# Attention heads on one core: TensorE makes the maxima's products, then the product of the weights with v, then the transposed scores

## The chip, the cores and the metric

The kernel runs on one core of a Trainium2 chip. The metric is device time in microseconds (us), lower is better. Five engines of the core matter: TensorE (PE, matrix products into PSUM), VectorE (DVE), ScalarE (ACT), GpSimd (POOL) and SyncE (SP, which issues the DMAs). Each works through its own list of instructions in order and waits on semaphores for the others. TensorE's clock has two levels here, 1.2 and 2.4 GHz; the profile gives the granted one as a share of full speed.

## What is computed

Two transformer-like layers over x of 4 x 1024 x 256, in float32, each half followed by a layer norm of x plus the half's output: a gated convolution with an MLP, a mixture of experts, an attention with block mask and rotary positions, and a gated MLP that keeps the two largest of each four hidden values. The change is in the attention alone:

```python
q = _rope(q)                      # (B=4, H=16, T=1024, D=16)
k = _rope(k)
scores = jnp.einsum('bhqd,bhkd->bhqk', q, k) * SCALE
scores = jnp.where(tok_mask[None, None], scores, -jnp.inf)   # blocks of 64, causal
attn = jax.nn.softmax(scores, axis=-1)
ctx = jnp.einsum('bhqk,bhkd->bhqd', attn, v)
ctx = ctx.transpose(0, 2, 1, 3).reshape(Bc, Tc, Cc)
return ctx @ w_o.T
```

## The kernel before

The program has three phases: convolution and MLP, experts, then attention and the last MLP. The third (`attention_ffn_phase`) handles the four sequences one after the other: `heads(b)` makes the attention of sequence b, then the output projection and the MLP of b follow, among which the projections and the first maxima of sequence b+1 are spread. Nothing of the MLP can begin before `heads(b)` has given the whole context.

In `heads(b)` the 16 heads are taken in four groups g = 0..3 of four heads. A group has 20 steps s, two for each of ten units of the score matrix (`UNITS`): the even step is heads 0 and 1 of the group (pair 0), the odd step heads 2 and 3. A unit is up to four blocks of 128 x 128; unit 2 (steps 4 and 5) and unit 9 (steps 18 and 19) are two blocks wide. Four kinds of work belong to a step:

- `scores(b, g, s)` (L1841): TensorE makes k times q, that is the transposed scores, for one pair, into the PSUM bank `W[s % 2]`. It waits (`exp_ok`) until ScalarE has read that bank two steps earlier. Scores are made one step ahead: in step s those of s+1.
- `exponentials(b, g, s)` (L1382): ScalarE takes exp of the bank and writes it to SBUF, into the unit's slot of `weights`.
- `weighted(b, g, u, part)` (L1861): TensorE multiplies v by the weights of unit u = s/2 - 1, for all four heads, and adds it up in the bank `O`. It is called in the even steps 2, 4 .. 18 for the unit whose second exp is that of step s-1, and waits for that exp. The last unit's product is made in step 0 of the next group, or after the loop in the last group. Here it is called "the product with v".
- `for_maxima` (L1814, L1817): q times k for another group, whose row maxima VectorE takes (`maximum`, L1543 and L1548). Two jobs in a step, through the two halves of the bank `X`; a job waits until VectorE has read its half. The jobs done in group g are those of group g+1, and from step 17 on those of g+2 (`max_jobs`). Group 0's own jobs are made ahead of `heads`, so group 2 has none after step 16 and group 3 has none at all.

In odd steps there is something more on TensorE: transposes of q and k rows of later groups (L1781), which ScalarE then copies out (L1372, L1376), or of the sums (`sums_transposed`, L1870), whose copy by ScalarE is L1388 (after exp 0 and exp 7) and which VectorE divides out.

The order is written out by hand. Before the change TensorE's step is: scores of s+1, two maxima jobs, the extra work of an odd step, and in an even step the product with v last. In step 0 it is already: product with v of the group before, maxima jobs, scores. ScalarE's order in a step is exp of s, then copies; it is not touched, nor is VectorE's.

Of the kernel before, what the change touches and what calls it, by code (L numbers as in the profile page):

```python
# [61 lines left out]
def wait(eng, sem, value):  # L62

    if not isinstance(value, int) or value > 0:
        eng.wait_ge(sem, value)  # L65
# [1036 lines left out]
NHG = HEADS // HG  # L1102
# [44 lines left out]
def attention_ffn_phase(nc, io, keep):  # L1147
    with ExitStack() as ctx:  # L1148
# [114 lines left out]
        def group(b, g):  # L1263

            return Step(None, 0, b * NHG + g)
# [5 lines left out]
        def max_jobs(g, s):  # L1271

            return (g + 1, AHEAD + 2 * s) if AHEAD + 2 * s < 2 * NX else (g + 2, AHEAD + 2 * s - 2 * NX)
# [477 lines left out]
        def _(pe):  # L1751
# [32 lines left out]
            def qk_transposed(b, g, pair, s):  # L1784
                rows_transposed(t_bank(g, pair, s), g, pair, s, kq_mm)

            def q_max_transposed(b, g, pair):
                wait(pe, nm_ok, group(b, g)(2, LEAD + pair + 1))
                rows_transposed(q_max_bank(g, pair), g, pair, 0, tm_mm)
# [33 lines left out]
            def for_maxima(b, g, low, high):  # L1823
                for m in range(low, high):
                    for_maximum(b, g, m)
# [47 lines left out]
            def heads(b):  # L1873
                scores(b, 0, 0)
                qk_transposed(b, 1, 0, 1)
                wait(pe, qm_ok, group(b, 0)(2, 1))
                qk_transposed(b, 1, 0, 0)
                for_maxima(b, 1, 0, AHEAD)
                q_max_transposed(b, 0, 1)
                for g in range(NHG):  # L1880
                    for s in range(STEPS):
                        of, m = max_jobs(g, s)
                        if s == 0 and g > 0:
                            weighted(b, g - 1, NU - 1, 0)
                        if s == 0 and of < NHG:
                            for_maxima(b, of, m, m + 2)
                        if s + 1 < STEPS:
                            scores(b, g, s + 1)
                        elif g + 1 < NHG:
                            scores(b, g + 1, 0)  # L1890
                        if s > 0 and of < NHG:
                            for_maxima(b, of, m, m + 2)
                        if s == 1 and g > 0:
                            wait(pe, qm_ok, group(b, g)(2, 2))
                            sums_transposed(b, g - 1, 1)
                        if s == 9:
                            if g + 1 < NHG:
                                wait(pe, kq_ok, group(b, g + 1)(4, 4))
                            elif g > 0:
                                wait(pe, cn_ok, group(b, g - 1)(2, LEAD + 2))  # L1900
                            sums_transposed(b, g, 0)
                        if g + 1 < NHG:
                            if s == 3:
                                if g > 0:
                                    wait(pe, cn_ok, group(b, g - 1)(2, LEAD + 2))
                                qk_transposed(b, g + 1, 1, 1)
                            if s == 5:
                                wait(pe, kq_ok, group(b, g + 1)(4, 3))
                                qk_transposed(b, g + 1, 1, 0)
                            if s == 11:  # L1910
                                wait(pe, cn_ok, group(b, g)(2, LEAD + 1))
                                q_max_transposed(b, g + 1, 0)
                        if g + 2 < NHG:
                            if s == 13:
                                wait(pe, qm_ok, group(b, g + 1)(2, 1))
                                qk_transposed(b, g + 2, 0, 1)
                            if s == 15:
                                wait(pe, kq_ok, group(b, g + 2)(4, 1))
                                qk_transposed(b, g + 2, 0, 0)
                        if s > 0 and s % 2 == 0:  # L1920
                            weighted(b, g, s // 2 - 1, 0)
                        if s > 0 and s % 2 == 0:
                            weighted(b, g, s // 2 - 1, 1)
                        if s == STEPS - 1 and g + 1 < NHG:
                            if g + 2 < NHG:
                                wait(pe, kq_ok, group(b, g + 2)(4, 2))
                            else:
                                wait(pe, qm_ok, group(b, g + 1)(2, 1))
                            q_max_transposed(b, g + 1, 1)
                weighted(b, NHG - 1, NU - 1, 0)  # L1930
                wait(pe, cn_ok, group(b, NHG - 1)(2, LEAD + 1))
                sums_transposed(b, NHG - 1, 1)
# [212 lines left out]
```

How the kernel before makes its waits and increments, by code:

```python
def wait(eng, sem, value):  # L62
    if not isinstance(value, int) or value > 0:
        eng.wait_ge(sem, value)
# [110 lines left out]
        def x_arrived(eng, n, par):  # L176
            if n.reg is None:
                eng.wait_ge(x_loaded[par], 16 * (n.off // 2 + 1))
            else:
                eng.wait_ge(x_loaded[par], n.reg * 16 + 16 * (n.off // 2 + 1))
# [1 line left out]
        @block.sync  # L183
# [11 lines left out]
            sp.dma_start(got_dn, io["w_dn"]).then_inc(dn_ld, 16)  # L195
            sp.dma_start(got_out, io["w_out"]).then_inc(out_ld, 16)
            for n, par in steps(sp, 2, ALL):
                if n.among(1, NG):
                    wait(sp, xx_ok, n(1))
                    load(n.before(-1), 1 - par)
                if n.among(1, NG + 1):
                    b = n.before(1)
                    wait(sp, xa_ok, b(1, 1))
                    sp.dma_start(io["rows_t"][:, tiles(b), 0:D], x2).then_inc(row_st, 16)
            sp.wait_ge(row_st, 16 * NG)
# [1 line left out]
        @block.gpsimd  # L207
        def _(pool):
            pool.memset(power[:], -0.5).then_inc(setup, 1)
            pool.memset(eps[:], 1e-5).then_inc(setup, 1)
            pool.wait_ge(setup, 2)
            def rms(n, ss_ok, ss, g, g_ok, rn, rn_ok, used):
# [7 lines left out]
            rms(Step(None, 0, 0), ss1_ok, ss1, g1, g1_ok, rn1, rn1_ok, h_ok)
            pool.wait_ge(wa_ok, 3)
            pool.tensor_tensor(w_up[1][:, :, :], got_up, w_up[0][:, :, :], ALU.subtract).then_inc(wp_ok, 1)
# [502 lines left out]
            def gather():  # L728
                pool.wait_ge(idx_ok, 1)
                pool.wait_ge(w_st, 16)
```

## Time and profile before

| | |
|---|---|
| median of 3 runs | 1879.51 us (1877.37 to 1886.38) |
| the profiled execution | 1887.31 us, its span 1885.2 us |
| TensorE busy | 1636.9 us (87%), mean granted clock 0.924 |
| VectorE busy | 1134.7 us (60%) |
| ScalarE busy | 798.1 us (42%) |
| steps of `heads`, four sequences, each | 116 to 117 us |

A row of the timeline is: start and length in us, engine, line, operation, what it writes and reads, shape, how many instructions were merged into the row, and in brackets the idle time of the engine before it with what ended it. PE is the matrix product itself, PEld the load of its fixed operand. ScalarE instructions overlap a little: one exp of full width lasts 1.02 us, and the next begins 0.9 us after the start of it. A row of the windows is: stretch, its length, then the busy time (and number of instructions) of PE, PEld, DVE, ACT and POOL, then the granted clock, the DMA share and GB/s.

### The profile page before, as it was taken

To read this page: it belongs to the slowest core of one execution; us is meant where nothing else is said; L and a number is where in the kernel's file an instruction comes from. 1 tells how busy PE (TensorE), PEld (TensorE's weight loads), DVE (VectorE), ACT (ScalarE), POOL (GpSimd) and SP (SyncE) were. 2 spreads that over 40 slices of the span, in tenths; PEclk is the share of its full clock that TensorE was granted. 3 is DMA by queue.
4 is the path that set the end of the run, shared out by engine and by line. 5 is a ranking of instruction groups with operands and counts; after the bars stand their busy time and mean duration, and the time that the engine had idled before them with its cause. 6 is when DMAs were issued, how large, how long until landed. Compare 5 with 4: busy or idle time off the path is not lost.

```text
span 1885.2 us, 26388 instructions
## 1 busy us (share of the span) xinstructions
PE 1636.9 (87%) x10042; PEld 1007.5 (53%) x10043; DVE 1134.7 (60%) x2355; ACT 798.1 (42%) x1308; POOL 236.0 (13%) x237
## 2 busy tenths in 40 slices
PE   3899999986989986688899989899888899899797
PEld 3788888874557774233355433355433455433355
DVE  5566566646421036767468677577677477677465
ACT  5444444421312221357643167552167552267430
POOL 4333333311320001000000000100000100000100
PEclk8999999987999888679999989999989899989999
DMA  2000000005014412000000000000000000000000
GB/s 103 12 23 23 22 22 22 22 12 178 16 35 139 130 56 92 1 1 1 1 1 1 0 1 1 24 1 1 1 1 1 23 1 1 1 1 1 23 1 23
DMA packets 27147, 47.96 MB, mean 25 GB/s; under 512 B 7312, under 2 KB 16016, under 8 KB 26256
## 3 DMA queue, kind: packets, MB, share of 16 engines
q1 hardware_dynamic: 26464, 44.74, 7.4%
q0 software_dynamic: 576, 1.77, 0.3%
q8 instruction: 70, 1.15, 0.3%
q14 instruction: 37, 0.30, 0.1%
HBM read 37.59 MB, written 9.06 MB: 25 GB/s over the span
## 4 chain that ended last, share of the span: by engine, by line
issue 59%; POOL 2%; DVE 0%; POOLq 0%; DVEq 0%
POOL rs_sb L1314 1%; POOL ve_sb L1311 0%; POOL qks_sb L1329 0%; POOL v_sb L1328 0%; DVE bn_sb L1491 0%; POOL qks_sb L1319 0%; DVE x_sb_sb L1506 0%; POOLq L1148 0%; POOLq L65 0%; POOL qks_sb L1330 0%; DVE mv_sb L1497 0%; DVEq L1148 0%; POOL v_sb L1327 0%; DVEq L65 0%; DVEq L1495 0%
## 5 line engine op out<-in xcount | busy, mean ns | idle before, releaser
L1548 DVE TENSOR_REDUCE mx_sb<-s_ps 128x1 f32<-128x512 f32 (+1 forms) x512 | 312.7, 652 | 145.1 <-PE s_ps L1817 84.7
L1382 ACT ACTIVATE room_sb<-s_ps 128x1024 f32<-128x1024 f32 (+1 forms) x320 | 280.9, 948 | 23.7 <-PE s_ps L1841 22.7
L1814 PE MATMUL s_ps<-room_sb 48*128 48x512 f16 (+3 forms) x640 | 176.2, 346 | 25.0 <-DVE mx_sb L1548 16.7
L1861 PE MATMUL cm_ps<-room_sb,v_sb 128*32 128x512 f32 (+3 forms) x1536 | 168.3, 529 | 0.8 <-ACT room_sb L1388 0.8
L1841 PE MATMUL s_ps<-room_sb 51*128 51x128 f16 (+4 forms) x1152 | 123.6, 287 | 41.8 <-ACT room_sb L1382 34.7
L1311 POOL TENSOR_TENSOR ve_sb<-mv_sb,eps_sb 128x4 f32<-128x4 f32 x24 | 5.1, 212 | 1114.4 <-DVE mv_sb L1497 1114.4
L1984 PE MATMUL cm_ps<-w_fd_sb,room_sb 128*128 128x256 f32 x512 | 130.7, 403 | 14.6 <-DVE room_sb L1627 14.6
L1841 PEld LDWEIGHTS s_ps<-room_sb 50*128 50x128 f16 (+1 forms) x1152 | 39.1, 96 | 182.1 <-ACT room_sb L1382 146.6
L1814 PEld LDWEIGHTS s_ps<-room_sb 48*128 48x128 f16 x640 | 54.4, 98 | 145.7 <-DVE mx_sb L1548 97.0
L1971 PE MATMUL s_ps<-xbT_sb,w_fg_sb 128*128 128x512 f32 x256 | 128.9, 615 | 0.8 <-ACT xbT_sb L1419 0.8
L1971 PE MATMUL s_ps<-xbT_sb,w_fu_sb 128*128 128x512 f32 x256 | 128.3, 613 | 0.0
L392 DVE SCALAR_TENSOR_TENSOR x_sb_sb<-xp_sb,conv_w_sb,x_sb_sb 128x512 f32<-128x512 f32 x96 | 108.5, 1139 | 22.8 <-ACT x_sb_sb L319 20.6
L1984 PEld LDWEIGHTS cm_ps<-w_fd_sb,room_sb 128*128 128x128 f32 x512 | 96.8, 197 | 39.2 <-DVE room_sb L1627 14.0
L398 DVE SCALAR_TENSOR_TENSOR m1T_sb<-mm_ps,m1T_sb 128x512 fp32r<-128x512 f32 x64 | 44.3, 692 | 97.2 <-ACT m1T_sb L311 97.2
L956 PE MATMUL em_ps<-xT_sb,ws_gu_sb 128*128 128x512 f32 x192 | 91.6, 623 | 8.0 <-DMA rows<-zeros 8.0
L1424 ACT ACTIVATE sgl_sb<-s_ps 128x512 f32<-128x512 f32 x64 | 38.2, 597 | 136.0 <-PE s_ps L1971 135.9
L1817 PE MATMUL s_ps<-room_sb 51*128 51x128 f16 x512 | 81.2, 235 | 9.6 <-ACT room_sb L1372 9.2
L1543 DVE TENSOR_REDUCE mx_sb<-s_ps 128x2 f32<-128x512 f32 (+1 forms) x128 | 66.3, 554 | 24.3 <-PE s_ps L1817 24.3
L479 PE MATMUL mm_ps<-h1T_sb,w_up_sb 128*128 128x512 f32 x128 | 57.6, 450 | 23.0 <-DVE h1T_sb L416 23.0
L311 ACT ACTIVATE m1T_sb<-mm_ps 128x512 fp32r<-128x512 f32 x64 | 38.1, 596 | 80.6 <-PE mm_ps L481 80.6
L479 PE MATMUL ro_ps<-w_dn_sb,m1T_sb 128*128 128x256 f32 x256 | 71.5, 279 | 0.0
L480 PE MATMUL ro_ps<-w_dn_sb,m1T_sb 128*128 128x256 f32 x256 | 71.5, 279 | 0.0
(245 smaller groups left out, 3237.6 us busy)
## 6 DMA issues: line engine op xcount, KB each, us to landing
we_gu_sb<-we_gu SPq DMA_DIRECT2D x32, 352.0 KB
we_dn_sb<-we_dn SPq DMA_DIRECT2D x32, 176.0 KB
x_in_sb<-x SPq DMA_DIRECT2D x9, 512.0 KB, 3.5
rows<-x_sb_sb SPq DMA_DIRECT2D x8, 512.0 KB, 3.0
x_sb_sb<-rows SPq DMA_DIRECT2D x2, 2048.0 KB, 11.6
out<-x_sb_sb SPq DMA_DIRECT2D x8, 512.0 KB, 2.6
xp_sb<-w_in SPq DMA_DIRECT2D x1, 1024.0 KB, 5.8
x_sb_sb<-w_up SPq DMA_DIRECT2D x1, 1024.0 KB, 7.0
```

The costliest lines, as they stand in the source:

```text
L392: dve.scalar_tensor_tensor(xc[:, c, :], xp[:, c, k:k + GTOK], conv_w[:, c, k:k + 1], xc[:, c, :], ALU.mult, ALU.add)\
L479: pe.matmul(out, of[0][at], by[0][cols], start=start, stop=False)
L480: pe.matmul(out, of[1][at], by[0][cols], start=False, stop=False)
L956: last = pe.matmul(mm[c % 4][:, :], ws_gu[:, k, col:col + P], xT[:, k, g * GTOK:(g + 1) * GTOK], start=(k == 0), stop=(k == KD - 1))
L1382: act.activation(weights[(g * NU + u) % SLOTS_P][:, 2 * pair:2 * pair + 2, 0:width(u) * P], W[s % 2][:, :, 0:width(u) * P], ACT.Exp, scale ...
L1548: dve.tensor_reduce(mx[:, pair, k % 2, slot:slot + 1], X[:, k % 2, 0:count * P], AX.X, ALU.max, negate=True).then_inc(mx_ok, 1)
L1814: last = pe.matmul(X[:, k % 2, at * P:(at + plain) * P], query[head:head + NORM, i * P:(i + 1) * P], key[head:head + NORM, j * P:(j + plai ...
L1817: last = pe.matmul(X[:, k % 2, (at + plain) * P:(at + count) * P], query[head:head + USED, i * P:(i + 1) * P], key[head:head + USED, i * P ...
L1841: last = pe.matmul(W[s % 2][:, head, (at + low - i) * P:(at + high - i) * P], key[first:first + rows, j * P:(j + 1) * P], query[first:firs ...
L1861: last = pe.matmul(O[32 * h:32 * h + 32, (i - half * GT) * P:(i - half * GT + count) * P], v[:, j, g * HG + h, :], weights[(g * NU + u) % ...
L1971: last = pe.matmul(bank[:, e, :], wt[:, k, ch * P:(ch + 1) * P], xbT[:, k, g * 512:(g + 1) * 512], start=(k == 0), stop=(k == KD - 1))
L1984: last = pe.matmul(CM[:, t // 2, (t % 2) * D:(t % 2 + 1) * D], hs[:, k % 3 * 4 + i, t * P:(t + 1) * P], w_fd[:, k % 2 * 4 + i, :], start=( ...
```

## The change

In every step s of `heads` TensorE's calls are put in one order: maxima jobs, then (in even steps after 0) the product with v, then the scores of the next step, then the extra work of the odd steps. No instruction is added or taken away, and no semaphore is changed; each wait stays with its instruction.

```diff
-                        if s == 0 and of < NHG:
+                        if of < NHG:
                             for_maxima(b, of, m, m + 2)
+                        if s > 0 and s % 2 == 0:
+                            weighted(b, g, s // 2 - 1, 0)
+                            weighted(b, g, s // 2 - 1, 1)
                         if s + 1 < STEPS:
                             scores(b, g, s + 1)
                         elif g + 1 < NHG:
                             scores(b, g + 1, 0)
-                        if s > 0 and of < NHG:
-                            for_maxima(b, of, m, m + 2)
...
-                        if s > 0 and s % 2 == 0:
-                            weighted(b, g, s // 2 - 1, 0)
-                        if s > 0 and s % 2 == 0:
-                            weighted(b, g, s // 2 - 1, 1)
```

TensorE in group 3, steps 8 to 14, before (L1841 the scores, two products a step at this width; L1861 the product with v; L1870 the transposed sums):

```order
L1861 MATMUL cm_ps<-room_sb,v_sb 32x512 x4
L1841 MATMUL s_ps<-room_sb 128x512 x2
L1870 MATMUL cm_ps<-ident_sb,room_sb 128x128 x4
L1841 MATMUL s_ps<-room_sb 128x512 x2
L1861 MATMUL cm_ps<-room_sb,v_sb 32x512 x4
L1841 MATMUL s_ps<-room_sb 128x512 x4
L1861 MATMUL cm_ps<-room_sb,v_sb 32x512 x4
```

and the same stretch of the change:

```order
L1861 MATMUL cm_ps<-room_sb,v_sb 32x512 x4
L1841 MATMUL s_ps<-room_sb 128x512 x4
L1870 MATMUL cm_ps<-ident_sb,room_sb 128x128 x4
L1861 MATMUL cm_ps<-room_sb,v_sb 32x512 x4
L1841 MATMUL s_ps<-room_sb 128x512 x4
L1861 MATMUL cm_ps<-room_sb,v_sb 32x512 x4
```

Both have two steps' scores between two products with v, but they are not the same scores: after the product of step s the list before goes on with the scores of s+2, that of the change with those of s+1.

TensorE at the start of `heads`, group 0, steps 1 and 2, before (L1814 and L1817 are a maxima job; the first three rows are the scores of step 2, made in step 1):

```order
L1841 MATMUL s_ps<-room_sb 128x128 x2
L1841 MATMUL s_ps<-room_sb 128x256 x2
L1841 MATMUL s_ps<-room_sb 128x128 x2
L1814 MATMUL s_ps<-room_sb 128x384
L1817 MATMUL s_ps<-room_sb 128x128
L1814 MATMUL s_ps<-room_sb 128x384
L1817 MATMUL s_ps<-room_sb 128x128
L1841 MATMUL s_ps<-room_sb 128x128 x2
```

and of the change, from the maxima jobs of step 1 on to the product with v of step 2:

```order
L1814 MATMUL s_ps<-room_sb 128x384
L1817 MATMUL s_ps<-room_sb 128x128
L1841 MATMUL s_ps<-room_sb 128x128 x2
L1841 MATMUL s_ps<-room_sb 128x256 x2
L1841 MATMUL s_ps<-room_sb 128x128 x2
L1814 MATMUL s_ps<-room_sb 128x384
L1817 MATMUL s_ps<-room_sb 128x128
L1814 MATMUL s_ps<-room_sb 128x384
L1817 MATMUL s_ps<-room_sb 128x128
L1861 MATMUL cm_ps<-room_sb,v_sb 32x512 x4
```

The maxima jobs of step 1 now stand ahead of the scores of step 2, and the product with v of step 2 stands ahead of the scores of step 3.

## Rows read from the trace of the kernel before

**Rows 1.** Windows of the four groups of the second sequence, and the sum of all 16.
```profile
1092.30:1126.50 34.20, 30.66 (x288) 12.02 (x288) 23.71 (x47) 23.42 (x27) 0.00 (x0) 0.85 0.01 2
1126.50:1159.90 33.40, 30.54 (x296) 12.56 (x296) 25.25 (x51) 23.94 (x29) 0.00 (x0) 0.90 0.01 1
1159.90:1189.50 29.60, 25.84 (x260) 10.17 (x260) 22.24 (x44) 22.07 (x27) 0.00 (x0) 1.00 0.00 1
1189.50:1208.40 18.90, 15.78 (x160) 4.90 (x164) 11.51 (x44) 18.03 (x23) 3.63 (x6) 1.00 0.14 57
...
sum 461.80, PE 408.93 PEld 158.16 DVE 321.45 ACT 349.63 POOL 11.68; mean PE 25.56 PEld 9.89 DVE 20.09 ACT 21.85 POOL 0.73
```
**Rows 2.** Waits of the whole run: who waited for whom, us, times, longest.
```profile
PE s_ps L1841 <- ACT room_sb L1382: 34.7, 84, 1.7
```
**Rows 3.** Timeline of group 3, second sequence.
```profile
1189.51 1.02 ACT L1382 ACTIVATE room_sb<-s_ps 128x1024 f32<-128x1024 f32 x1
...
1190.89 3.86 ACT L1382 ACTIVATE room_sb<-s_ps 128x1024 f32<-128x1024 f32 x5
...
1194.04 1.07 PE L1861 MATMUL cm_ps<-room_sb,v_sb 128*32 128x384 f32 x16
...
1195.05 0.60 PE L1841 MATMUL s_ps<-room_sb 50*128 50x512 f16 x4
1195.48 1.94 ACT L1382 ACTIVATE room_sb<-s_ps 128x1024 f32<-128x1024 f32 x2 [0.72 <-PE s_ps L1841]
...
1197.47 0.39 PE L1841 MATMUL s_ps<-room_sb 50*128 50x512 f16 x2 [0.53 <-ACT room_sb L1382]
1197.78 10.61 ACT L1382 ACTIVATE room_sb<-s_ps 128x1024 f32<-128x1024 f32 x12
...
1209.25 0.60 ACT L1388 ACTIVATE room_sb<-cm_ps 128x512 f32<-128x512 f32 x1 [0.86 <-PE cm_ps L1861]
```
**Rows 4.** Timeline of the end of group 2.
```profile
1185.27 1.06 PE L1861 MATMUL cm_ps<-room_sb,v_sb 128*32 128x512 f32 x8
...
1186.27 0.40 PE L1841 MATMUL s_ps<-room_sb 51*128 51x128 f16 x8
...
1186.60 1.08 ACT L1382 ACTIVATE room_sb<-s_ps 128x512 f32<-128x512 f32 x2 [1.26 <-PE s_ps L1841]
...
1187.93 0.62 PE L1781 MATMUL cm_ps<-ident_h_sb,qks_sb 128*128 128x128 f16 x8
...
1188.59 1.02 ACT L1376 ACTIVATE room_sb<-cm_ps 128x1024 f16<-128x1024 f16 x1 [0.91 <-PE cm_ps L1781]
```
**Rows 5.** Timeline of the first steps of group 0.
```profile
1093.36 0.61 PE L1841 MATMUL s_ps<-room_sb 51*128 51x128 f16 x6 [1.73 <-ACT room_sb L1382]
...
1094.27 0.61 PE L1841 MATMUL s_ps<-room_sb 51*128 51x128 f16 x6
1094.42 2.68 DVE L1548 TENSOR_REDUCE mx_sb<-s_ps 128x1 f32<-128x512 f32 x4 [3.03 <-PE s_ps L1817]
...
1096.30 1.93 PE L1861 MATMUL cm_ps<-room_sb,v_sb 128*32 128x512 f32 x8
```
**Rows 6.** Timeline of the first steps of group 2.
```profile
1162.42 0.40 PE L1841 MATMUL s_ps<-room_sb 51*128 51x128 f16 x6 [0.20 <-ACT room_sb L1382]
...
1163.34 1.06 PE L1861 MATMUL cm_ps<-room_sb,v_sb 128*32 128x512 f32 x8
```
**Rows 7.** Timeline of group 2, steps 4 to 6.
```profile
1166.54 1.07 PE L1861 MATMUL cm_ps<-room_sb,v_sb 128*32 128x384 f32 x16
...
1168.18 2.48 DVE L1548 TENSOR_REDUCE mx_sb<-s_ps 128x1 f32<-128x512 f32 x4 [0.65 <-PE s_ps L1814]
...
1169.84 0.64 PE L1861 MATMUL cm_ps<-room_sb,v_sb 128*32 128x256 f32 x8
```
**Rows 8.** Two stretches of group 0, columns as in Rows 1.
```profile
1099.20:1106.00 6.80, 5.72 (x62) 2.48 (x60) 5.88 (x13) 5.12 (x7) 0.00 (x0) 1.00 0.00 0
1106.00:1109.40 3.40, 3.40 (x24) 1.03 (x21) 1.46 (x3) 2.19 (x4) 0.00 (x0) 0.50 0.00 0
```

## The prediction, made before the changed kernel ran

> **What bounds the kernel now.** I read the busy times by group of heads first, then the list of waits, then the timeline of the places where the order changes. The heads take 461.8 us of the span in 16 groups, and groups 0 to 2 are not alike group 3 [rows 1]. In groups 0 to 2 TensorE is busy 87 to 91% of the time and sets the pace together with VectorE: where the products for the maxima are full width, TensorE makes two, VectorE reduces them, and TensorE can make the next two only as VectorE frees the halves. One such turn, from one product with v to the next, takes 3.30 us, in which VectorE does four reductions in 2.48 us [rows 7]. In group 3 there are no maxima. There ScalarE is busy 18.03 of 18.90 us [rows 1], and its exps stand nearly end to end [rows 3]: a pair of exps, 1.8 us, is the period of two steps. So group 3 is bound by ScalarE, as long as TensorE gives it scores in time.
>
> **Part 1, group 3: the scores come behind the product with v.** The units of cost are in [rows 3]. A full exp lasts 1.02 us and the next follows 0.9 us after its start (two in 1.94); a half-wide one takes 0.5 and lasts 0.6. TensorE starts scores 0.05 us after the exp it waits for has ended (1195.48 + 1.94 = 1197.42, then 1197.47). The product with v holds TensorE for 1.0 us (1194.04 to 1195.05); unit 2's, half as wide, I take at 0.57 (eight such instructions last 0.64 us where the wide ones last 1.07 [rows 7]). From scores to the exp on them it is 0.43 us where they stand right behind a product (1195.05 to 1195.48), and 0.31 us where TensorE was idle (1197.47 to 1197.78).
>
> In an even step s both the product and the scores of s+1 wait for the exp of s-1. Before, the scores go first, are ready 0.05 + 0.31 = 0.36 us after that exp, and the exp of s covers this; the product comes while ScalarE works. After the change the exp of s+1 can start only 0.05 + 1.0 + 0.43 = 1.48 us after the end of the exp of s-1, that is 1.02 + 1.48 = 2.50 us after its start, where ScalarE would be free after 1.80. So 0.7 us are added in each even step of full width. TensorE works in order, so nothing behind the product can serve ScalarE meanwhile.
>
> Walked through from the group's first exp at 0 (the second at 1.38, as in [rows 3], since a copy stands between them): exp 3 starts at 3.90, exp 5 at 6.41, exp 7 at 8.07 (small product), exp 9 at 11.08 (with the copy after exp 7), then every 2.50: 13.58, 16.08, 18.58, 21.08; exp 19 at 23.59 because the exp of step 18 is half as wide and covers less. It ends at 24.19. Before, the last copy begins 0.86 us after the last exp; now the product of unit 8 is out of its way, and I take 0.77: copy at 24.96, against 19.74 before (1209.25 less 1189.51). The group grows by **5.2 us**. The small waits before (0.72 us at one place) are inside this difference.
>
> **Part 2, the end of group 2.** From step 17 on there are no maxima there either. Counted from the product of step 16 (1185.27), the next group's first exp comes at 4.24 [rows 3, 4]. After the change: scores 17 at 1.0, exp 17 from 1.43 to 2.45, product with v of step 18 at 2.50 (before at once behind scores 18 and 19, at 1.33), scores 19 at 3.50, the next group's first scores at about 3.7, transposes at 4.0, their copy 0.66 later as before, 4.66, and the exp 0.92 behind it: 5.58. That is **1.3 us** more. Between groups 0 and 1, and 1 and 2, the maxima still fill this place; only one set of scores more stands ahead of the transposes, whose copy the next group waits for: about 0.25 us each, **0.5 us** together.
>
> **Part 3, the starts of the groups: a gain.** In step 1 scores 2 wait for exp 0, and the maxima jobs behind them wait too. At the start of group 0 this is large: TensorE idles 1.73 us before scores 2, and VectorE idles 3.03 us [rows 5]. After the change the maxima go ahead into this gap, VectorE has freed the halves when step 2 wants them, and the product with v of step 2 waits only for exp 1, which scores 3 follow today at 1094.27. It starts there and not at 1096.30: 2.0 us at most; I take **1.8 us**, since the rest of the stretch is then held by VectorE. In groups 1 and 2 the same step has the product at 1163.34, 0.92 us after scores 3 [rows 6]. It can gain 0 to 0.9; I take 0.5, because the sums' transposes and VectorE's division stand there: **1.0 us** for both.
>
> **Part 4, the rest of groups 0 to 2: nothing.** With maxima of full width the turn is: product, maxima pair, extra work and scores, first and second job of the next pair as VectorE frees them, product. Only the scores and the extra work change places, and their sum is hidden behind the reductions. Scores s+1 now stand behind the product, but their exp has the whole next 3.30 us turn to be ready in [rows 7]: it ends some 1.0 + 0.43 + 1.02 = 2.45 us after the product's start. If that cover were gone it would cost what group 3 pays, 0.7 us a turn. All waits of TensorE's scores for exps come to 34.7 us over the whole run [rows 2], so what could be won by hiding them is small, and a part of it lies in group 3, where it wins nothing.
>
> **Sum.** Per sequence 5.2 + 1.3 + 0.5 - 1.8 - 1.0 = +4.2 us, and four sequences 16.8 us. The heads are serial with what follows (the context must be whole), so it goes to the end unshortened. The profiled execution, 1887.3 us with a span of 1885.2, would be 1904; it lies 0.4% above the median of the runs, 1879.5, to which I add the same: **1896 us**.
>
> **Rivals.** *Faster.* The busiest engine of the heads is TensorE, 408.9 of 461.8 us, ScalarE only 349.6 [rows 1]. If TensorE is the bound throughout, letting independent maxima go before waiting scores wins back idle time. Groups 0 to 2 have 3.5 + 2.9 + 3.8 = 10.2 us of idle TensorE a sequence. This wins if more than 9.3 of these go, against the 2.8 I count (5.2 + 1.3 + 0.5 = 7.0 are lost, plus 2.3 to pass 0.5% over four sequences); all gone gives 4 x (7.0 - 10.2) = -13 us, 1867. Against it: most of that idle time is VectorE's turn. Chance 0.04. The Trainium skill, in "Perfetto Trace Analysis", section "Identifying the Most-Contended Engine", says to find the bound by occupancy and to optimise the busiest engine first; by that rule taken over the whole heads this change serves the right engine and the time falls. Taken group by group its occupancies agree with me: ScalarE leads in group 3.
>
> *Little change.* The terms on both sides come out at their kind ends: scores behind a product reach ScalarE after 0.31 and not 0.43 (ten places, 1.2 us less), the group borders between 0, 1 and 2 cost nothing, the starts gain 2.0 + 0.9 + 0.9. Then 4.0 + 1.3 - 3.8 = 1.5 a sequence, 6 us, 1885.5. Chance 0.14, with all that stays under 0.5%.
>
> *Much slower, by the clock.* In group 0 the granted clock falls to half from 1106.0 to 1109.4, after a stretch in which TensorE was busy 5.72 of 6.80 us [rows 8], and eight instructions of the product then take 1.93 us [rows 5] and not 1.06. Group 3 runs at full clock with 15.8 of 18.9 us busy (84%); changed, it would have the same work in some 24 us, 66%. If the clock falls in it, each product costs 0.87 more and the scores some 0.15, all on the path. With a third of its ten turns at half clock that is 3.4 us a sequence, 14 us in all: 1910. Chance 0.14. The Trainium skill, in "TensorE: Matmul & The Clock Gate", section "HAM oscillation", ties the fall to long idle gaps of TensorE; by it gaps of under 1.5 us as here would not bring the clock down and this rival would be out. The trace does not bear it out, since the fall of [rows 8] has no long gap before it; so I leave it its chance.
>
> **How the numbers follow.** Forecast (16.8 us, with terms off by a third to either side) 0.68; clock 0.14; little change 0.14; faster 0.04. A measurement of this kernel tells about 0.5%, 9.4 us, from no change. The range goes from 1885, the kind ends, to 1911, the clock's case. Slower by over 0.5% is forecast plus clock, 0.82; within 0.5% 0.14; faster 0.04.
>
> **What would show it.** Group 3 should take 24 us from first to last exp and not 18.9, with a wait of about 0.7 us for L1841 ahead of every second exp, and ScalarE at some 75% there; group 2 about 0.8 us longer, groups 0 and 1 about 1.6 and 0.3 shorter, and VectorE's 3.03 us wait at the start of group 0 mostly gone. If group 3's exps still stand end to end, part 1 is wrong; if groups 0 and 1 grow, or shrink by several us, part 4 is.

## The result: 0.3% slower, and where the time went

The changed kernel takes 1887.05 us (median of 20 runs, 1879.71 to 1896.07), the kernel before, on the same chip, 1881.35 us (20 runs). The ratio is 1.0032, with a 95% interval of 1.0018 to 1.0045: slower, by about 6 us and not by the 16.8 forecast, and within 0.5%. The time lies inside the range, the sign is right, and the size is little more than a third of the forecast. The profiled execution took 1881.48 us, with a span of 1879.4. Two timed runs of the whole study, one of the kernel before (2010.36 us) and one of e2 (2109.18 us), fell in a slower state and are left out of every median and ratio.

The page of the changed kernel, busy time by engine, and one group of instructions (the transposed scores):

```profile
PE 1619.0 (86%) x10042; PEld 999.1 (53%) x10043; DVE 1136.7 (60%) x2355; ACT 807.5 (43%) x1308; POOL 236.1 (13%) x237
...
L1841 PE MATMUL s_ps<-room_sb 51*128 51x128 f16 (+4 forms) x1152 | 121.8, 285 | 14.5 <-ACT room_sb L1382 7.3
```

The waits of the whole run (who waited for whom, us, times, longest), where one row has moved most:

```profile
ACT room_sb L1382 <- PE s_ps L1841: 98.3, 129, 1.9
...
PE cm_ps L1861 <- ACT room_sb L1382: 29.2, 40, 1.0
...
PE s_ps L1841 <- ACT room_sb L1382: 7.3, 8, 1.3
```

Before, the first row read 22.7 us, 26 times. ScalarE now waits 98.3 us for scores; 23.5 us of this lie in the four groups 3, where it waited 2.8 us before. TensorE waits for exps as long as it did, 29.2 + 7.3 = 36.5 us against the 34.7 of [rows 2], but now mostly in front of the product with v, for which the list of before has no such row, and the scores stand behind that product.

The windows of the four groups of the second sequence and the sum of all 16, as in [rows 1] (us; busy time and instructions of PE, PEld, DVE, ACT, POOL; granted clock; DMA share; GB/s):

```profile
1089.40:1120.40 31.00, 27.75 (x284) 11.45 (x284) 23.61 (x47) 23.98 (x28) 0.00 (x0) 0.93 0.01 2
1120.40:1151.00 30.60, 28.38 (x296) 12.07 (x296) 25.47 (x51) 24.64 (x30) 0.00 (x0) 1.00 0.01 1
1151.00:1181.20 30.20, 26.05 (x260) 10.35 (x260) 22.25 (x44) 22.60 (x28) 0.00 (x0) 1.00 0.00 1
1181.20:1205.30 24.10, 15.58 (x164) 4.99 (x164) 13.56 (x52) 18.64 (x23) 4.83 (x8) 1.00 0.11 45
...
sum 472.80, PE 402.08 PEld 158.83 DVE 328.25 ACT 359.44 POOL 14.47; mean PE 25.13 PEld 9.93 DVE 20.52 ACT 22.47 POOL 0.90
```

Group 3 has gone from 18.9 to 24.1 us at full clock, with ScalarE at 18.64 of 24.1 (77%). Group 2 went from 29.6 to 30.2 and group 1, at full clock, to 30.6 from 31.0. The heads as a whole take 472.8 us where they took 461.8 (116.4, 116.1, 113.5 and 116.1 for the four sequences, where the table of the time before says 116 to 117). The mechanism is there, then, yet the whole program gained back a large part. The timeline of group 3 shows the mechanism at its clearest:

```profile
1193.33 1.06 PE L1861 MATMUL cm_ps<-room_sb,v_sb 128*32 128x512 f32 x8 [0.32 <-ACT room_sb L1382]
1194.32 0.61 PE L1841 MATMUL s_ps<-room_sb 50*128 50x512 f16 x4
1194.76 1.94 ACT L1382 ACTIVATE room_sb<-s_ps 128x1024 f32<-128x1024 f32 x2 [0.57 <-PE s_ps L1841]
1195.83 1.07 PE L1861 MATMUL cm_ps<-room_sb,v_sb 128*32 128x512 f32 x8 [0.90 <-ACT room_sb L1382]
1196.83 0.61 PE L1841 MATMUL s_ps<-room_sb 50*128 50x512 f16 x6
1197.26 1.94 ACT L1382 ACTIVATE room_sb<-s_ps 128x1024 f32<-128x1024 f32 x2 [0.57 <-PE s_ps L1841]
```

Product, scores, two exps, a gap of 0.57 us, and again: from 1193.33 to 1195.83 it is 2.50 us a turn, to the hundredth what the prediction worked out. (The gap is 0.57 us and not 0.7 because the two exps beside it last 1.94 us, not 1.80.) In [rows 3] twelve exps stood end to end there.

The same at the start of group 0, against [rows 5]:

```profile
1088.58 0.53 PE L1814 MATMUL s_ps<-room_sb 48*128 48x384 f16 x2
...
1089.24 1.29 DVE L1548 TENSOR_REDUCE mx_sb<-s_ps 128x1 f32<-128x512 f32 x2 [0.70 <-PE s_ps L1817]
1089.43 2.85 ACT L1382 ACTIVATE room_sb<-s_ps 128x1024 f32<-128x1024 f32 x3
...
1090.51 0.61 PE L1841 MATMUL s_ps<-room_sb 51*128 51x128 f16 x6 [1.30 <-ACT room_sb L1382]
...
1091.47 1.93 PE L1861 MATMUL cm_ps<-room_sb,v_sb 128*32 128x512 f32 x8
1091.58 1.29 DVE L1548 TENSOR_REDUCE mx_sb<-s_ps 128x1 f32<-128x512 f32 x2 [1.05 <-PE s_ps L1817]
```

The maxima jobs of step 1 now run at 1088.58, before scores 2 wait; VectorE's wait of 3.03 us has become two, of 0.70 and 1.05, with two reductions between them, and the product of step 2 comes 2.04 us after exp 0 (1091.47 less 1089.43), where it came 4.0 after it (1096.30 less 1092.3).

### The profile page after: what moved, and what is told of

Read it like the earlier page. It is cut to its first block, busy times and chain, and to the rows that moved or that the text cites. A ratio compares the mean times of both kernels' runs of the same rounds, so it can differ in the third digit from the quotient of the medians.

```text
span 1879.4 us, 26388 instructions
## 1 busy us (share of the span) xinstructions
PE 1619.0 (86%) x10042; PEld 999.1 (53%) x10043; DVE 1136.7 (60%) x2355; ACT 807.5 (43%) x1308; POOL 236.1 (13%) x237
## 4 chain that ended last, share of the span: by engine, by line
issue 59%; POOL 2%; DVE 0%; POOLq 0%; DVEq 0%
POOL rs_sb L1314 1%; POOL ve_sb L1311 0%; POOL qks_sb L1329 0%; POOL v_sb L1328 0%; POOL qks_sb L1319 0%; DVE bn_sb L1491 0%; DVE x_sb_sb L1506 0%; POOLq L1148 0%; POOLq L65 0%; POOL qks_sb L1330 0%; DVE mv_sb L1497 0%; DVEq L1148 0%; POOL v_sb L1327 0%; DVEq L65 0%; DVEq L1495 0%
## 5 line engine op out<-in xcount | busy, mean ns | idle before, releaser
L1382 ACT ACTIVATE room_sb<-s_ps 128x1024 f32<-128x1024 f32 (+1 forms) x320 | 291.0, 939 | 98.7 <-PE s_ps L1841 98.3
L1814 PE MATMUL s_ps<-room_sb 48*128 48x512 f16 (+3 forms) x640 | 176.4, 345 | 33.0 <-DVE mx_sb L1548 16.4
L1861 PE MATMUL cm_ps<-room_sb,v_sb 128*32 128x512 f32 (+3 forms) x1536 | 165.7, 520 | 35.5 <-ACT room_sb L1382 29.2
L1311 POOL TENSOR_TENSOR ve_sb<-mv_sb,eps_sb 128x4 f32<-128x4 f32 x24 | 5.0, 210 | 1113.8 <-DVE mv_sb L1497 1113.8
L1814 PEld LDWEIGHTS s_ps<-room_sb 48*128 48x128 f16 x640 | 54.0, 97 | 163.6 <-DVE mx_sb L1548 98.7
L1841 PE MATMUL s_ps<-room_sb 51*128 51x128 f16 (+4 forms) x1152 | 121.8, 285 | 14.5 <-ACT room_sb L1382 7.3
L1841 PEld LDWEIGHTS s_ps<-room_sb 50*128 50x128 f16 (+1 forms) x1152 | 45.3, 97 | 133.8 <-ACT room_sb L1382 60.2
L1817 PE MATMUL s_ps<-room_sb 51*128 51x128 f16 x512 | 83.0, 233 | 10.1 <-ACT room_sb L1372 9.2
L1543 DVE TENSOR_REDUCE mx_sb<-s_ps 128x2 f32<-128x512 f32 (+1 forms) x128 | 66.2, 554 | 22.8 <-PE s_ps L1817 22.7
L1861 PEld LDWEIGHTS cm_ps<-room_sb,v_sb 128*32 128x32 f32 x1536 | 34.8, 111 | 84.0 <-ACT room_sb L1382 49.9
L479 PE MATMUL ro_ps<-w_dn_sb,m1T_sb 128*128 128x256 f32 x256 | 71.6, 280 | 0.0
```

Of the source, the lines that this page charges most:

```text
L479: pe.matmul(out, of[0][at], by[0][cols], start=start, stop=False)
L1382: act.activation(weights[(g * NU + u) % SLOTS_P][:, 2 * pair:2 * pair + 2, 0:width(u) * P], W[s % 2][:, :, 0:width(u) * P], ACT.Exp, scale ...
L1543: dve.tensor_reduce(mx[:, pair, k % 2, at:at + ST + 1:ST], X[:, k % 2, 0:2 * count * P].rearrange("p (a c) -> p a c", a=2), AX.X, ALU.max, ...
L1814: last = pe.matmul(X[:, k % 2, at * P:(at + plain) * P], query[head:head + NORM, i * P:(i + 1) * P], key[head:head + NORM, j * P:(j + plai ...
L1817: last = pe.matmul(X[:, k % 2, (at + plain) * P:(at + count) * P], query[head:head + USED, i * P:(i + 1) * P], key[head:head + USED, i * P ...
L1841: last = pe.matmul(W[s % 2][:, head, (at + low - i) * P:(at + high - i) * P], key[first:first + rows, j * P:(j + 1) * P], query[first:firs ...
```

## Experiments: which piece costs and which piece gains

All edits are against the kernel before, unless it says otherwise. The conditions are written here in their simplest form. Ratios are to the kernel before on the same chip, with 95% intervals. Lengths "at full clock" are of groups in which the granted clock reads 1.00; the time at half clock (1.2 GHz) in a stretch is twice its length times what the unrounded clock lacks of 1.

### e1: the maxima go first, the product stays last

```diff
-                        if s == 0 and of < NHG:
+                        if of < NHG:
                             for_maxima(b, of, m, m + 2)
                         if s + 1 < STEPS:
                             scores(b, g, s + 1)
                         elif g + 1 < NHG:
                             scores(b, g + 1, 0)
-                        if s > 0 and of < NHG:
-                            for_maxima(b, of, m, m + 2)
```

> One part of the change alone: the maxima jobs of steps 1 to 19 go ahead of the scores; the product with v stays last in its step. Theory A (the two parts add up; the loss sits where the product with v stands ahead of the scores and there are no maxima, the gain where maxima jobs no longer wait behind scores): group 3 as before, 18.9 us from first exp to end, group 2 not longer than before (29.6 us), groups 0 and 1 shorter by some 2 and 0.5 us at full clock, so about 1868 us (ratio 0.993) or less if the clock falls less often too. Theory B (groups 0 to 2 gained because the product with v moved, not the maxima): ratio 1.000.

Measured: 1861.37 us against 1882.8, ratio 0.9888 (0.9861 to 0.9915). No kernel of the study is faster (e5 below is level with it within the intervals); it is 1.1% faster than the one before and, by the two ratios, 1.4% faster than the full change. The windows of its groups 1 to 3, second sequence:

```profile
1122.00:1152.50 30.50, 28.31 (x296) 11.98 (x296) 25.50 (x51) 24.13 (x30) 0.00 (x0) 1.00 0.01 2
1152.50:1181.60 29.10, 25.98 (x260) 10.23 (x260) 22.25 (x44) 22.36 (x28) 0.00 (x0) 1.00 0.00 1
1181.60:1200.40 18.80, 15.73 (x158) 4.85 (x162) 11.48 (x44) 17.94 (x23) 3.62 (x6) 1.00 0.14 58
```

Group 3 is as before, group 2 half a microsecond shorter than the 29.6 of [rows 1], group 1 half shorter than its 31.0. All that the full change gains is in the half of it that moves the maxima.

### e2: the product goes first, the maxima stay behind the scores

```diff
                         if s == 0 and of < NHG:
                             for_maxima(b, of, m, m + 2)
+                        if s > 0 and s % 2 == 0:
+                            weighted(b, g, s // 2 - 1, 0)
+                            weighted(b, g, s // 2 - 1, 1)
                         if s + 1 < STEPS:
                             scores(b, g, s + 1)
...
-                        if s > 0 and s % 2 == 0:
-                            weighted(b, g, s // 2 - 1, 0)
-                        if s > 0 and s % 2 == 0:
-                            weighted(b, g, s // 2 - 1, 1)
```

> The other part alone: the product with v goes ahead of the scores in the even steps, the maxima jobs stay behind the scores. Theory A: group 3 takes 24.1 us instead of 18.9, the end of group 2 about 1 us more, groups 0 and 1 keep their starting gap; ratio 1.012 to 1.015 (about 1905 us). Theory B: group 3 loses the same 5.2 us, but groups 0 and 1 win back 2 to 3 us each, ratio 1.003 to 1.006.

Measured: 1970.41 us, ratio 1.0484 (1.0446 to 1.0522), three to four times the loss expected. So the two halves of the change don't add. The timeline of group 0, second sequence, shows why:

```profile
1142.02 1.07 PE L1861 MATMUL cm_ps<-room_sb,v_sb 128*32 128x512 f32 x8
...
1143.25 0.38 PE L1814 MATMUL s_ps<-room_sb 48*128 48x512 f16 x2
1143.66 2.48 DVE L1548 TENSOR_REDUCE mx_sb<-s_ps 128x1 f32<-128x512 f32 x4 [1.37 <-PE s_ps L1814]
1144.12 0.40 PE L1841 MATMUL s_ps<-room_sb 51*128 51x128 f16 x6 [0.49 <-ACT room_sb L1382]
1144.41 0.39 PE L1814 MATMUL s_ps<-room_sb 48*128 48x512 f16 x1
1145.01 0.39 PE L1814 MATMUL s_ps<-room_sb 48*128 48x512 f16 x1 [0.21 <-DVE mx_sb L1548]
...
1145.88 1.07 PE L1861 MATMUL cm_ps<-room_sb,v_sb 128*32 128x512 f32 x8
```

The turn is 3.86 us (1142.02 to 1145.88), and was 3.31 in this group and 3.30 in group 2 [rows 7]. The product now stands where no reduction covers it: the maxima pairs of steps s and s+1 follow each other with scores alone between them, VectorE has nothing to reduce during the product (its idle of 1.37 us before 1143.66, where [rows 7] has 0.65), and TensorE waits in the pairs. In the full change the maxima ahead of the product fill VectorE during it. Part 4 of the prediction, "nothing" for the inner turns, holds for the two moves made together, and not for this one alone.

### e3: the full change where a step has maxima, the old order where it has none

```diff
-                        if s == 0 and of < NHG:
+                        if of < NHG:
                             for_maxima(b, of, m, m + 2)
+                        if s > 0 and s % 2 == 0 and of < NHG:
+                            weighted(b, g, s // 2 - 1, 0)
+                            weighted(b, g, s // 2 - 1, 1)
...
-                        if s > 0 and s % 2 == 0:
+                        if s > 0 and s % 2 == 0 and not of < NHG:
                             weighted(b, g, s // 2 - 1, 0)
-                        if s > 0 and s % 2 == 0:
                             weighted(b, g, s // 2 - 1, 1)
```

> The full change where a step has maxima jobs (groups 0, 1 and 2 up to step 16), the order of before where it has none (group 2 from step 17, group 3). Theory A: group 3 is 18.9 us again and group 2 about 1 us shorter than in the full change, so 4 x (5.2 + 0.9) = 24 us under the full change: ratio 0.990 to the kernel before, about 1862 us, faster than both. If the loss of the full change sits elsewhere: ratio 1.003 as the full change.

Measured: 1868.04 us, ratio 0.9924 (0.9904 to 0.9944). The loss is gone and the gain stays, so the loss is where no maxima stand. One detail missed: group 2 did not shorten with the old order from step 17 on.

```profile
1148.00:1178.30 30.30, 26.16 (x260) 10.34 (x260) 22.21 (x44) 22.49 (x28) 0.00 (x0) 1.00 0.00 1
1178.30:1197.10 18.80, 15.73 (x158) 4.85 (x162) 11.49 (x44) 17.94 (x23) 3.62 (x6) 1.00 0.15 58
```

Group 3 is back at 18.8, but group 2 takes 30.3, as in the full change, where e1 has 29.1. The timeline of e3 at the end of group 2:

```profile
1172.61 1.06 PE L1861 MATMUL cm_ps<-room_sb,v_sb 128*32 128x512 f32 x8
...
1174.05 2.01 ACT L1382 ACTIVATE room_sb<-s_ps 128x1024 f32<-128x1024 f32 x3 [1.37 <-PE s_ps L1841]
...
1178.25 1.02 ACT L1382 ACTIVATE room_sb<-s_ps 128x1024 f32<-128x1024 f32 x1
```

Step 16 still has maxima, so its product is still ahead of scores 17, and ScalarE idles 1.37 us until exp 17 starts 1.44 us behind that product. From the product to the next group's exp 0 it is 5.64 us, against 4.24 before [rows 3, 4]. The whole loss of part 2 is decided by this one pair, not by the steps behind it as my walk suggested.

### e4: the product ahead in group 3 alone

```diff
+                        if s > 0 and s % 2 == 0 and g == NHG - 1:
+                            weighted(b, g, s // 2 - 1, 0)
+                            weighted(b, g, s // 2 - 1, 1)
                         if s + 1 < STEPS:
                             scores(b, g, s + 1)
...
-                        if s > 0 and s % 2 == 0:
+                        if s > 0 and s % 2 == 0 and g < NHG - 1:
                             weighted(b, g, s // 2 - 1, 0)
-                        if s > 0 and s % 2 == 0:
                             weighted(b, g, s // 2 - 1, 1)
```

> The order of before everywhere but in group 3, where the product with v goes ahead of the scores as in the full change. Theory A: group 3 24.1 us and everything else as before, so 4 x 5.2 = 21 us more, ratio 1.011. If the clock falls in group 3 because TensorE idles there: more than 1.015 and a granted clock below 1 in that group in more than one of the four sequences. If the gain of the full change in groups 0 and 1 came from what group 3 does to the clock: under 1.008.

Measured: 1899.08 us, ratio 1.0087 (1.0061 to 1.0113), 16 us, for a part that should cost 4 x 5.2 = 21 less what the program gives back. Its group 3 in two of the sequences:

```profile
1192.10:1217.40 25.30, 17.03 (x164) 5.38 (x164) 13.65 (x52) 18.68 (x23) 4.82 (x8) 0.93 0.11 43
...
911.90:936.00 24.10, 15.57 (x164) 4.99 (x164) 7.51 (x28) 18.60 (x23) 2.41 (x4) 1.00 0.00 1
```

24.1 us at full clock, which is part 1 of the prediction by itself (24.19). In two sequences the clock fell in this group, for 3.4 and 2.7 us, and it took 25.3 and 25.0.

### e5: the maxima ahead of the scores in step 1 alone

```diff
-                        if s == 0 and of < NHG:
+                        if s <= 1 and of < NHG:
                             for_maxima(b, of, m, m + 2)
...
-                        if s > 0 and of < NHG:
+                        if s > 1 and of < NHG:
                             for_maxima(b, of, m, m + 2)
```

> Only in step 1 of each group the maxima jobs go ahead of the scores. The forecast's own part 3 says that all of the gain of the maxima jobs is there: about 1.8 + 0.5 + 0.5 us a sequence, so group 0 some 2 us shorter and about the same time as with all maxima jobs ahead (ratio 0.989 to 0.994). Rival: the gain comes in equal bits from all steps in which scores waited; then group 0 is shorter but groups 1 and 2 are as before at full clock (31.0 and 29.6 us), ratio 0.995 or more.

Measured: 1864.08 us, ratio 0.9905 (0.9886 to 0.9923), most of e1's gain from one step in each group. Its groups of the third sequence:

```profile
1359.70:1391.40 31.70, 28.35 (x284) 11.90 (x284) 23.62 (x46) 23.34 (x28) 0.00 (x0) 0.89 0.00 1
1391.40:1422.00 30.60, 28.10 (x297) 12.02 (x296) 25.46 (x50) 23.84 (x29) 0.00 (x0) 1.00 0.01 1
1422.00:1451.20 29.20, 25.89 (x263) 10.22 (x260) 22.49 (x44) 22.03 (x27) 0.00 (x0) 1.00 0.01 2
```

Groups 1 and 2 are 0.4 us shorter at full clock, each. Group 0 is some 0.8 us shorter at like time at half clock (31.9 us with 7.4 at half clock, against 32.8 with 7.8 before), not the 2 us expected. So the groups themselves give about 4 x 1.5 = 6 of the 17 us, and the rest goes with a higher clock (median 0.934 to 0.935 over the timed runs, against 0.927). In none of the eight occurrences of groups 1 and 2 did the clock fall in this one profile, while in the kernel before it falls in 13 of 32 of them over four profiled executions.

### e6: in group 3, half of the product ahead of the scores, half behind

```diff
-            def weighted(b, g, u, part):
+            def weighted(b, g, u, part, heads=range(HG)):
...
-                for h in range(HG):
+                for h in heads:
...
+                        if s > 0 and s % 2 == 0 and g == NHG - 1:
+                            for part in range(len(WEIGHTED[s // 2 - 1])):
+                                weighted(b, g, s // 2 - 1, part, range(HG // 2))
                         if s + 1 < STEPS:
                             scores(b, g, s + 1)
...
+                        if s > 0 and s % 2 == 0 and g == NHG - 1:
+                            for part in range(len(WEIGHTED[s // 2 - 1])):
+                                weighted(b, g, s // 2 - 1, part, range(HG // 2, HG))
```

> Only in group 3: two of the four heads' products with v go ahead of the scores, the other two behind them; all else as before. If the four heads' products run one after the other (0.25 us each), the scores come 0.5 us earlier than with the whole product ahead, a turn is 2.0 us, group 3 takes some 20.5 us, ratio 1.003 to 1.004. If the four run side by side in the array, two take nearly as long as four (1.0 us each half), the turn is 2.5 us or, since TensorE then needs 2.6 us a turn, more: group 3 24 to 25 us, ratio 1.010 or more.

Measured: 1898.89 us, ratio 1.0093 (1.0079 to 1.0107). Group 3 takes 25.7 us, more than with the whole product ahead and above the 24 to 25 expected. TensorE's timeline there:

```profile
1202.69 1.05 PE L1861 MATMUL cm_ps<-room_sb,v_sb 128*32 128x512 f32 x4
1203.67 0.39 PE L1841 MATMUL s_ps<-room_sb 50*128 50x512 f16 x2
1203.99 1.05 PE L1861 MATMUL cm_ps<-room_sb,v_sb 128*32 128x512 f32 x4
1204.98 0.39 PE L1841 MATMUL s_ps<-room_sb 50*128 50x512 f16 x2
1205.30 1.05 PE L1861 MATMUL cm_ps<-room_sb,v_sb 128*32 128x512 f32 x4
```

Four instructions take 1.05 us where the eight of all four heads take 1.06: each half holds TensorE as long as the whole, and the turn is 2.61 us, with TensorE now the bound. The half meant to halve the delay doubled the time that TensorE spends on products. This run doesn't say whether a delay of 0.5 us would have been free.

### r1 and r2: the full change and the kernel before, once more

No edit.

> The full change once more, unaltered, for a second profile and a ratio on another chip. Theory A (without the clock the change costs what was forecast, some 14 us in the heads; the rest of the difference is TensorE time at the low clock, elsewhere): group 3 again 24.1 us and group 1 30.5 us, the parts that the change does not touch between 1395 and 1425 us in sum, the granted clock above that of the kernel before. Theory C (the first profile was only lucky outside the heads): those parts as long as in the kernel before, ratio near 1.007.

> The kernel before once more, unaltered. Theory A: clock about 0.926, lower than the full change's on the same chip by some 0.005; the parts outside the heads again about 1423 us in this profile. Theory C: clock and those parts as in the full change.

Measured: the full change 1884.0 us, ratio 1.0015 (1.0000 to 1.0030); the kernel before, as a candidate beside itself, 1879.27 us, ratio 0.9989 (0.9974 to 1.0004). The forecast of +0.9% is excluded again, so its miss is no accident of one compilation or chip. In the two profiles the heads are 473.6 and 460.5 us and all the rest of the program 1407.9 and 1420.9, close to the first two (1406.6 and 1423.2).

### n1 to n4: edits that change nothing in the order of the heads

The stretch ahead of the first heads, which the change doesn't touch, was 815.7 and 817.6 us in the two profiles of the kernel before and 809.7 and 809.3 in those of the full change. Four neutral edits ask whether that comes with the change. n1 (kernel before) and n3 (full change) swap two waits that TensorE makes together:

```diff
             def out_projection(b):
-                wait(pe, cTv_ok, b + 1)
                 wait(pe, cTa_ok, b + 1)
+                wait(pe, cTv_ok, b + 1)
```

n2 (kernel before) and n4 (full change) repeat a wait that is already met:

```diff
             pe.wait_ge(ready, 1)
+            pe.wait_ge(ready, 1)
```

> The kernel before with two waits of TensorE, both long before the output projection's first product, written in the other order: nothing that takes time is changed. Theory D (the stretch ahead of the heads, whose code no kernel here changes, takes 809 to 811 us or 816 to 818 us by how the program happens to lie against the clock or in memory): the stretch jumps to the other level, 7 us less, with this or the next edit, ratio 0.995 to 1.000. Rival: the stretch is tied to the order in the heads; then 816 to 818 us and ratio 1.000.

> The kernel before with one wait more on TensorE, on a semaphore that has already been met, before the first rows' transposes: all later instructions lie one place further in memory. Theory D: 809 to 811 us ahead of the heads is possible, heads as before (460 to 462 us). Rival: 816 to 818 us and ratio 1.000.

> The full change with the two waits in the other order. Theory D: 809 to 811 us ahead of the heads as in the two profiles of the full change, or 816 to 818; heads 473 us. If the low level belongs to the order in the heads: 809 to 811 us, ratio 1.002 to 1.004.

> The full change with the one wait more. Theory D: the stretch ahead of the heads may jump to 816 to 818 us, ratio then near 1.006. If the low level belongs to the order in the heads: 809 to 811 us, ratio 1.002 to 1.004.

Measured: n1 0.9977 (0.9953 to 1.0002), n2 1.0000 (0.9976 to 1.0023), n3 1.0033 (1.0008 to 1.0058), n4 1.0052 (1.0026 to 1.0077). The windows of this stretch, in the kernel before and in n1:

```profile
0.00:815.70 815.70, 683.00 (x3950) 546.90 (x3951) 409.54 (x869) 272.29 (x578) 207.88 (x181) 0.89 0.17 52
```

```profile
0.00:809.70 809.70, 678.00 (x3950) 542.67 (x3951) 408.12 (x869) 272.12 (x578) 207.85 (x181) 0.90 0.17 53
```

The same 3950 matrix products take 6 us less with two waits swapped in a place that comes later; n2 has 809.5, n3 810.3 and n4 809.4. So the kernel before can have the short stretch too, and the order of the heads alone does not decide this level. It is a matter of the clock: by the records, 177 and 180 us of the stretch are at half clock in the long ones, 163 and 164 in the short ones. Whether the build or the single execution sets the level is not shown, since each build has one profile. The timed runs speak for the execution: the profiled one of n1 (1871.17 us) lies 8 us under the median of its own kernel, and 6 us, a ratio of 0.9968, lie outside the interval of n2, though inside that of n1.

## Why the forecast of the mechanism was right and its size was not

**The terms, one by one.** All lengths at full clock, per sequence, from the first exp of a group to the first of the next:

| | forecast | measured |
|---|---|---|
| group 0 (-1.8 and +0.25) | -1.55 | about -1.2 |
| group 1 (-0.5 and +0.25) | -0.25 | -0.46 (31.00 to 30.54) |
| group 2 (-0.5 and +1.3) | +0.8 | +0.63 (29.57 to 30.20) |
| group 3 | +5.2 | +5.24 (18.88 to 24.12) |
| sum | +4.2 | +4.2 |

Group 0 is never at full clock all through; the figure compares groups with like time at half clock: 34.2 us with 10.5 us before and 33.0 with 10.4 in r1, 35.5 with 14.0 in r2 and 34.4 with 14.3 after. Part 1 holds to 0.1 us, and e4 shows it alone. Part 2: 5.54 us from the product of step 16 (at 1175.64) to the next exp 0 (at 1181.18), forecast 5.58. Part 3 holds in kind and is somewhat too large for group 0: 2.0 us earlier at the start, of which about 1.2 last to the end of the group, and e5 shows that step 1 alone brings most of it. The 0.25 us for each border between groups is in these sums; no run shows it by itself. Part 4 holds for the full change and, as e2 shows, only because both moves are made together.

**What failed: "the heads are serial with what follows, so it goes to the end unshortened".** Serial they are, but something else also stood in the way behind them. Part of a layer norm ends there on VectorE (L1506, with GpSimd's L1311 and L1314 ahead of it). The timeline of the kernel before, behind the last exp of the second sequence:

```profile
1209.61 1.01 POOL L1314 TENSOR_TENSOR rs_sb<-ve_sb,power_sb 128x4 f32<-128x4 f32 x1
1209.99 0.63 PE L1870 MATMUL cm_ps<-ident_sb,room_sb 128*128 128x128 f32 x4 [0.81 <-ACT room_sb L1388]
...
1210.73 1.38 DVE L1506 TENSOR_SCALAR x_sb_sb<-x_sb_sb,mv_sb,rs_sb 128x256 f32<-128x256 f32 x4 [1.48 <-POOL rs_sb L1314]
...
1212.03 0.25 DVE L1577 RECIPROCAL rc_sb<-cm_ps 128x16 f32<-128x16 f32 x1
```

and of the changed kernel:

```profile
1202.71 1.05 DVE L1506 TENSOR_SCALAR x_sb_sb<-x_sb_sb,mv_sb,rs_sb 128x256 f32<-128x256 f32 x3
...
1206.80 0.63 PE L1870 MATMUL cm_ps<-ident_sb,room_sb 128*128 128x128 f32 x4 [0.81 <-ACT room_sb L1388]
...
1207.46 0.26 DVE L1577 RECIPROCAL rc_sb<-cm_ps 128x16 f32<-128x16 f32 x1 [3.70 <-PE cm_ps L1870]
```

Before, the sums were ready at 1210.62, but VectorE waited 1.48 us for GpSimd, then normed for 1.38, and the division came at 1212.03, 3.64 us after the last exp. In the longer group 3 the norm is over before the last exp, and the division comes right behind the sums, 2.16 us after it. Over the four profiles of the full change this happens in seven of eight second and third sequences; over the four of the kernel before the delay is 3.51 us on the mean. That is 1.2 us back in each of these two sequences and 0.1 in each of the others (the product of unit 8 out of the way, as forecast), some 2.7 us in all. The rows POOL 3.63 (x6) in [rows 1] and 4.83 (x8) above are this work moving into group 3. It can be read also from e1, e3 and e5, where group 3 is short and the delay is 3.6 us in five of six such places; in e6, with a long group 3, it is 2.24 in both. I took the end of the heads for one chain and did not ask what else stands on VectorE there. The rows were there in the trace of before.

**What failed second, and weighs more: "to which I add the same".** Of the 11 us that are missing (16.8 less 5.7) VectorE explains 2.7, and the clock some 8. The sum was made at the clock as it was. The table gives the means of the four profiled executions of each kernel (the first, the repeat and the two with neutral edits), in brackets the time at half clock:

| us | kernel before | full change | difference |
|---|---|---|---|
| ahead of the first heads | 813.1 (170.9) | 809.7 (163.4) | -3.4 |
| four sequences of heads | 460.0 (59.5) | 472.0 (43.5) | +12.0 |
| what follows each | 604.0 (39.4) | 598.1 (36.0) | -5.9 |
| span | 1877.1 | 1879.8 | +2.7 |

The +2.7 us are less than the 6 of the timed runs: the profiled executions of the full change and of n4 lie 6 and 8 us under the medians of their own kernels. The table serves to see where the time lies, not how much it is.

In groups 1 and 2 the clock fell in 13 of 32 cases before ([rows 1] has one, group 1 at 0.90) and in 2 of 32 after. At half clock for 6.8 us group 1 takes 33.4 us and not 31.0, so 1 us at half clock costs 0.35 us here. The heads have 16 us less of it, worth some 5: that is why 16.8 appeared as 12.0. I had a rival for the clock, but on one side only, a fall in group 3. It did occur: in 3 of 16 groups 3 after, each then some 2 us longer (26.2 for 24.1), and also in 3 of 16 before, each 0.8 us longer. Its net price over a run is 1 us, not 14. The prediction set the rule of the Trainium skill's section "HAM oscillation" (falls with long idle gaps) against [rows 8], and the trace still speaks against that rule here. The Trainium skill's page "TensorE: Matmul & The Clock Gate" has another one, in "A second HAM failure mode: psum-queue depth-cycling": in another kernel, short idle stretches between groups of products, often enough, also made the clock swing. This case agrees with that one as far as it goes: before the falls in groups 1 and 2 of the kernel before, TensorE was at work with idle stretches of 0.52 us at most, in all four profiles. With the maxima of step 1 moved the falls there are fewer, 5 in 56 groups (the full change, e1, e3 and e5) against 17 in 48 without (the kernel before, e4 and e6); but groups of one execution resemble each other, e4 and e6 have only 2 in 8 each, as e3 has, and what in the first steps brings the falls on was not tried.

**The timed runs say the same.** Nearly every timed run has its mean granted clock on record. Over 104 runs of the kernel before (the neutral edits n1, n2 and the repeat among them) the median is 1880.2 us at a mean clock of 0.928; over the 56 of the full change 1886.3 at 0.933. A straight line through each set gives, at a clock of 0.930, 1876.4 and 1890.3 us: 14 us at equal clock. The forecast terms less what VectorE gave back are 16.8 - 2.7 = 14.1. The slopes are -1.7 and -1.4 us for each 0.001, so that the mean clock, higher by 0.005, gives some 8 us back, and 6 are left, which is what the medians show. That a kernel at equal clock would be 14 us slower is an arithmetic of two sets of runs; the clock can't be held, so it is not an experiment. Nor does the higher clock need the moved maxima: e6 touches group 3 alone, and its four groups, 27.2 us longer, less 2.8 on VectorE would give 24 us, where 18 were measured at a median clock of 0.932 against 0.927.

**What stays open.** Of the -5.9 us in what follows the heads, 2.7 are VectorE's. The 3.4 us less at half clock there are worth 1.2 us at the 0.35 from above (an estimate), so that about 2 us are without a cause. Whether the change brings about the fewer microseconds at half clock, or whether they differ from execution to execution as ahead of the heads, the runs don't tell. The same holds for the -3.4 us ahead of the heads in four profiles each.

**The rivals.** *Faster*, with TensorE as the bound: false for the full change, but half true. It is e1, where only the independent maxima go ahead of waiting scores, and it gains 1.1%. Its heads take 443.9 us against the mean of 460.0; some 9 of these 16 us are shorter groups at equal clock (4 x (1.2 + 0.6 + 0.5)), and the rest goes with 22 us less at half clock. The product with v is the wrong thing to put ahead, since it waits for the same exp as the scores and takes 1 us. *Little change* came nearest in time, 1885.5 against 1887.05, for the wrong reason, so its time was luck: its kind ends did not come true. The scores reached ScalarE 0.43 to 0.44 us after they began and not 0.31, and the 2.0 us won at the start of group 0 shrank to 1.2 by its end.

## What to carry to other kernels

Where two pieces of work wait for the same event, the one that feeds the next engine goes first, and only work that is independent of the event may stand ahead of both: the maxima ahead gained 1.1%, about half of it through the clock, the product ahead cost 5.24 us a group where ScalarE was the bound. A time worked out at one place arrives at the end less what else was late there; look at every engine at the border behind it, not only at those on the chain. And where the clock swings, give an estimate for it in both directions, and compare timed runs at equal clock before a term is called wrong.

## What the runs showed of the hardware

- The product of v for four heads (each 32 columns of the array) takes 1.06 us for eight instructions and 1.05 for four (e6): the heads' instructions run side by side, and to halve such a product by heads saves no time.
- The mean granted clock of one and the same kernel varies from run to run, 0.921 to 0.937 for the kernel before, and each 0.001 goes with 1.4 to 1.7 us of 1880.
- A stretch whose code is the same in all kernels but for the harmless wait of n2 and n4 took 809 to 811 us in ten profiles and 816 to 818 in four, with 163 to 167 or 176 to 180 us at half clock in it. What sets this is not shown.
- Scores reach ScalarE 0.43 to 0.44 us after they begin behind a product (1194.32 to 1194.76, 1196.83 to 1197.26), as in [rows 3], with another order around them.
